# A DLRM tower on one core: products written to HBM in 136-byte pieces and read back whole, instead of written whole and read back in 136-byte pieces

## The reference, cut to what matters

```python
e = stack([tbl_f[ids[:, f]] for f in range(26)], axis=1)      # B, 26, 64
x = layer_norm(dense_t @ Wd.T, gd, bd)                        # B, 128
y = layer_norm(einsum('bnd,ed->bne', e, Ws), gs, bs)          # B, 26, 128
y = layer_norm(einsum('bne,pn->bep', y, Wsi), gsi, bsi)       # B, 128, 32
T = concatenate([x[:, None, :], swapaxes(y, 1, 2)], axis=1)   # B, 33, 128
Z = einsum('bnd,bmd->bnm', T, T)                              # B, 33, 33
z = layer_norm(Z[:, TRIL_I, TRIL_J] @ Wl.T, gl, bl) * mask    # B, 512, first 384 in use
h = maximum(concatenate([z, r_dense_t], 1) @ W_top1 + b_top1, 0)
y = maximum(h @ W_top2 + b_top2, 0) @ W_top3                  # B, 1
```

## Time and profile before

| what | us |
|---|---|
| median of 3 runs | 965.37 |
| lowest and highest run | 953.86 and 973.7 |
| span of the profiled execution, first to last instruction | 583.2 |
| PE busy in it | 520.8 |
| PE weight loads busy | 438.6 |
| DVE busy | 443.4 |
| POOL busy | 398.6 |
| ACT busy | 273.3 |

### The profile page before, as it was taken

One profiled execution on the slowest core, in us unless ns is written; L12 is line 12 of the kernel. 1 busy time (PEld: TensorE's weight loads), 2 busy tenths in 40 slices (PEclk: granted clock), 3 DMA queues, 4 the chain that ended last, 5 costly groups with the idle time before them and its releaser, 6 DMA issues.

```text
span 583.2 us, 19038 instructions
## 1 busy us (share of the span) xinstructions
PE 520.8 (89%) x7293; PEld 438.6 (75%) x7293; DVE 443.4 (76%) x862; ACT 273.3 (47%) x647; POOL 398.6 (68%) x420
## 2 busy tenths in 40 slices
PE   2469689999999999999998989999998999899786
PEld 1456568888787878887797868788787878788575
DVE  5488888888787878787787878787887888787611
ACT  1124354544545463645554464645545454646321
POOL 6777776777777777777777777777777777774000
PEclk9988989999999999999999999999999999999889
DMA  3534435454444436354543545354544444353410
GB/s 90 154 121 125 58 64 68 72 64 74 52 70 61 63 64 65 63 66 72 56 70 58 65 63 65 64 66 72 56 68 63 64 67 56 65 70 52 47 23 2
DMA packets 97305, 39.04 MB, mean 67 GB/s; under 512 B 77313, under 2 KB 89217, under 8 KB 97281
## 3 DMA queue, kind: packets, MB, share of 16 engines
q1 hardware_dynamic: 83970, 25.07, 30.7%
q0 software_dynamic: 13312, 13.66, 13.5%
HBM read 29.76 MB, written 8.92 MB: 66 GB/s over the span
## 4 chain that ended last, share of the span: by engine, by line
POOL 56%; issue 19%; DMA 10%; PE 10%; DVE 2%; ACT 1%; SPq 0%; POOLq 0%; DVEq 0%; ACTq 0%
POOL rows L452 56%; DMA rows<-in_table,index 10%; PE p_y L463 2%; PE p_u L541 1%; PE p_b L463 1%; PE p_b L480 1%; PE p_z L613 1%; PE p_b L485 1%; PE p_b L482 1%; PE p_t L516 0%; PE p_q L552 0%; PE p_y L577 0%; DVE ut_low L1000 0%; PE p_q L701 0%; PE p_y L670 0%
## 5 line engine op out<-in xcount | busy, mean ns | idle before, releaser
L452 POOL DMA_INDIRECT rows<-in_table,index x416 | 398.4, 958 | 134.0 <-issue 122.9
L541 PEld LDWEIGHTS p_u<-wsi_c,rows_n 128*128 128x128 f32 x512 | 83.3, 195 | 2.8
L1046 DVE TENSOR_TENSOR feat<-p_y,y_rs 128x1024 f32<-128x1024 f32 x64 | 78.4, 1225 | 9.1 <-DVE y_rs L1043 3.7
L1033 DVE TENSOR_REDUCE y_sum<-y_sq 128x32 f32<-128x1024 f32 x64 | 77.9, 1217 | 6.5 <-ACT y_sq L800 2.3
L541 PE MATMUL p_u<-wsi_c,rows_n 128*128 128x192 f32 (+4 forms) x512 | 82.8, 306 | 0.0
L1000 DVE TENSOR_TENSOR ut_low<-p_u,ut_high 128x512 fp32r<-128x512 f32 x64 | 44.1, 689 | 32.3 <-ACT ut_high L751 32.1
L800 ACT ACTIVATE y_sq<-p_y 128x1024 f32<-128x1024 f32 x64 | 64.8, 1012 | 3.3 <-PE p_y L581 3.3
L552 PE MATMUL p_q<-gram,et 128*128 128x128 f32 x416 | 60.4, 285 | 2.7 <-ACT et L738 2.7
L738 ACT COPY et<-p_t 128x512 f32<-128x512 f32 (+1 forms) x64 | 32.2, 504 | 63.5 <-PE p_t L516 61.4
L613 PEld LDWEIGHTS p_z<-feat 128*32 128x32 f32 x4096 | 47.6, 111 | 16.8 <-issue 12.3
L613 PE MATMUL p_z<-feat 128*32 128x34 f32 x4096 | 57.4, 201 | 0.1
(11 more groups left out here) (140 smaller groups left out, 854.2 us busy)
## 6 DMA issues: line engine op xcount, KB each, us to landing
products<-zs SPq DMA_DIRECT2D x64, 136.0 KB
zb<-products SPq DMA_DIRECT2D x256, 34.0 KB
rows<-in_table,index POOLq DMA_INDIRECT x416
dense_x<-in_dense SPq DMA_DIRECT2D x16, 128.0 KB
wl<-in_Wl_rows SPq DMA_DIRECT2D x1, 1280.0 KB, 6.5
w<-in_W SPq DMA_DIRECT2D x2, 512.0 KB
masks<-in_masks SPq DMA_DIRECT2D x1, 960.0 KB, 6.7
w1z<-in_W SPq DMA_DIRECT2D x1, 768.0 KB, 4.5
```

The costliest lines, as they stand in the source:

```text
L452: pool.indirect_dma_start(out=rows[:, j, g, :], out_offset=None, in_=a["table"], in_offset=bass.IndirectOffsetOnAxis(ap=index[:, n, t, g % ...
L541: last = nc.tensor.matmul(p_u[:, NP * (lo - UH * of):NP * (hi + 1 - UH * of)], rows_n[:, t, :, :].rearrange("r h d -> r (h d)"), wsi_c[:, ...
L1033: nc.vector.tensor_reduce(y_sum[:], y_sq[:], AX, ALU.add).then_inc(y_summed, 1)
L1046: nc.vector.tensor_tensor(feat[:, (j - 1) % UB, :, 2:SLOTS], p_y[:].rearrange("e (b p) -> e b p", p=NP), y_rs[:].unsqueeze(2).to_broadcast ...
```

## The change

The samples of a batch get another order: sample 32 u + 4 g + s of a batch is now sample (g, s) of unit u. A unit's 32 samples are then 32 neighbouring partitions of `zb`. `scratch` gets the shape (batch, unit, g, 128, 34), so that a sample's 32 rows of 34 floats lie together in HBM. The read back of a unit is one DMA of 32 pieces of 4,352 bytes in place of four DMAs of 256 pieces of 136 bytes. The store of a unit, 128 pieces of 1,088 bytes before, becomes 1,024 pieces of 136 bytes. ACT's wait on `zb_in` counts 16 a batch and quarter in place of 64, its copy of x to `feat` goes in the new order, and the host orders `ids` to match.

```diff
-    scratch = nc.dram_tensor("products", (NB, 128, GB, SLOTS), F32, kind="Internal").ap()
+    scratch = nc.dram_tensor("products", (NB, UB, GU, 128, SLOTS), F32, kind="Internal").ap()
...
             def read_quarter(of, quarter):
 
                 sp.sem_inc(read_begun, 1)
-                for s in range(SQ):
-                    at = 32 * s + GU * quarter
-                    sp.dma_start(plain[at:at + GU],
-                                 scratch[of, 32 * s:32 * s + 32, GU * quarter:GU * quarter + GU, :].rearrange("p g c -> g p c")
-                                 ).then_inc(zb_in[quarter], 16)
+                sp.dma_start(zb[SU * quarter:SU * quarter + SU, 0:ZROW],
+                             scratch[of, quarter].rearrange("g (s p) c -> (g s) (p c)", s=SQ)).then_inc(zb_in[quarter], 16)
...
-                        sp.dma_start(scratch[of, :, GU * quarter:GU * quarter + GU, :],
+                        sp.dma_start(scratch[of, quarter].rearrange("g r c -> r g c"),
                                      zs[:, j % 2]).then_inc(z_stored[j % 2], 16)
...
                         for quarter in range(UB):
-                            act.wait_ge(zb_in[quarter], 64 * i)
+                            act.wait_ge(zb_in[quarter], 16 * i)
...
-                        nc.scalar.copy(feat[:].rearrange("e u (s g) c -> e c s u g", s=SQ)[:, 0],
-                                       p_a[:, 128:256].rearrange("e (s u g) -> e s u g", s=SQ, u=UB)).then_inc(xt_ready, 1)
+                        nc.scalar.copy(feat[:].rearrange("e u (s g) c -> e c u g s", s=SQ)[:, 0],
+                                       p_a[:, 128:256].rearrange("e (u g s) -> e u g s", s=SQ, u=UB)).then_inc(xt_ready, 1)
...
-    ids = x["ids"].reshape(NB, 2, 2, UB, GU, NF).transpose(0, 1, 3, 2, 4, 5).reshape(NB, 2, NT, 128).transpose(3, 0, 2, 1)
+    ids = x["ids"].reshape(NB, UB, GU, 2, 2, NF).transpose(0, 3, 1, 4, 2, 5).reshape(NB, 2, NT, 128).transpose(3, 0, 2, 1)
```

## The result

The changed kernel takes **987.98 us** (median of 4 runs, 983.56 to 990.93), the kernel before 968.26 us (4 runs beside it, 953.86 to 973.7). The ratio is **1.028, 95% interval 1.020 to 1.035**: slower, by about 20 us. 962 was forecast and 982 was the range's upper end, so time and direction were both missed. A ratio in this document is that of each kernel's faster runs, those within 1.5% of its quickest, so it can differ from the ratio of the medians.

A forecast was written before the change was run, and what follows sets the result against it. The prediction took POOL's gather pace as the bound. From the 583.2 us span it took 2.8 us of POOL's waits and 0.3 at the end, giving 580.1, and carried 382.2 us outside: 962 us, range 948 to 982.

The forecast's parts named there:

- What bounds the kernel now: First step: POOL's gathers, at least 1.249 us apart, set 98% of the time up to 531.9 us.
- the 382 us: Time between the 583.2 us span and the timed median, taken to lie outside the span and carried unchanged.
- It can give POOL at most 4.5 us: Bound on what changed DMA queues could save POOL in late gathers in the steady part: 4.5 us.
- Reads, 0.5 us: Read back of a unit as 4,352-byte pieces: 0.5 us of transfer in place of 3.0, not on the path by itself.
- Stores, 3.0 us: Store of a unit as 1,024 pieces of 136 bytes: taken as 3.0 us, between 0.5 and 6.0.
- SP's queue, 4.4 us from store to read: SP's wait between a unit's store and read grows from 1.94 to 4.4 us, at no cost.
- The end, hidden: Last store and read land at 560.1, hidden by 3.4 us behind ACT's L718, which ends at 563.48.
- POOL's waits for landings below 5 us: Sign in the profile after: POOL's idle for DMA at its gathers, line 449, below 5 us in total.
- Rival 3: Small HBM writes are slow, hold DMA engines and make gathers late: 14 to 109 us, middle 1025 us; chance 0.10.
- Rival 2: New stores run earlier in each turn and may meet waited-for gathers: 14 us more, 979 us; chance 0.12.
- Rivals 1 and 4: POOL's waits come from elsewhere, nothing gained, 965 us, chance 0.22; or more comes back, some 10 us, 955 us, 0.08.
- Rival 5: The read's 4,352-byte pieces are cut small again, so DMA bursts double: 979 us; chance 0.03.

The follow-up runs named there:

- e3: Changed kernel with its new small-piece store but the four old small reads a unit, products permuted: 943.25 us, ratio 1.038 to the kernel before (921.12).
- e4: Changed kernel with the old store of 1,088-byte pieces and the new large read, products permuted: 998.38 us, ratio 1.103 to the kernel before.
- e5: Kernel before with one matmul a unit in place of its 64 products, transfers unchanged: 852.7 us (unedited kernel before 921.12).
- e8: Kernel before with two added waits, on POOL's gathers and PE's products, that keep gathers and products apart: 849.23 us (without them 918.55).
- e1: Kernel before, unedited, timed and profiled again: 974.82 us (934.6 to 993.73, 10 runs).
- e10: Old store with the new large read in the changed kernel, as e4, run again in another group: 990.21 us (kernel before 918.55).
- e12: Changed kernel plus the four old small reads a unit into an unused tile, with ACT waiting for them too: 951.02 us (kernel before 969.23).
- e14: Changed kernel with one added wait: POOL starts a unit's gathers only after the products two units back: 791.56 us, ratio 0.821 to the kernel before.
- e6: Changed kernel with one matmul a unit in place of its 64 products, transfers unchanged: 837.35 us (unedited kernel before 921.12).
- e7: Changed kernel with two added waits, on POOL's gathers and PE's products, that keep gathers and products apart: 827.89 us (kernel before 918.55).

## Why the prediction was wrong

**The step that failed is the first: "What bounds the kernel now".** "98% of the time up to 531.9 us is POOL's own pace" is true of the execution in the earlier trace rows and of no timed one. The sign was in the table: 583.2 us of span against a 965 us median. I wrote that "the 382.2 us between span and median hold no instruction that changes, so I carry them". Every later run shows 1.8 to 1.9 us outside the span. The prediction named both halves of this as what would prove it wrong, the 382 us and a PE that "loses time that I have not seen". In the timed executions POOL stands still for 511 us before its gathers, 385 of them for a DVE result, PE idles 253 us before the products, and what counts is how much of PE's work falls in bursts of gathers.

**"It can give POOL at most 4.5 us"** was the bound of the gain for the same wrong regime. For the loss the prediction said "What it can take is not bounded this way", and that is where the +20 us went: through the large read, to PE's crawl (e3, e4 and the sign that turns in e5 to e8), a path that no term of the sum had. How the large read does it stays open.

**Sizes of the parts**, by rows of the changed kernel. SP's queue in the steady part, then the last store and read; ACT's copy at the end; the end's windows (the last two columns are DMA share and GB/s):

```profile
447.44 0.41 SPq L387 DMA_DIRECT2D products<-zs  x1
...
451.64 0.32 SPq L371 DMA_DIRECT2D zb<-products  x1
```

```profile
958.18 0.40 SPq L387 DMA_DIRECT2D products<-zs  x1
962.11 0.31 SPq L371 DMA_DIRECT2D zb<-products  x1
```

```profile
965.29 1.14 ACT L715 ACTIVATE h<-p_y,b1z 128x128 f32<-128x128 f32 x4 [4.88 <-PE p_y L460]
966.31 1.26 ACT L754 COPY zc<-zb 128x576 f32<-128x576 f32 x1
```

```profile
959.00:959.50 0.50, 0.16 (x1) 0.16 (x2) 0.29 (x1) 0.00 (x0) 0.00 (x0) 1.00 0.68 112
959.50:960.00 0.50, 0.39 (x3) 0.15 (x2) 0.00 (x0) 0.07 (x1) 0.00 (x0) 1.00 0.92 153
960.00:960.50 0.50, 0.00 (x0) 0.00 (x0) 0.00 (x0) 0.41 (x1) 0.00 (x0) 1.00 0.10 14
960.50:962.00 1.50, 1.45 (x13) 1.48 (x14) 0.00 (x0) 0.00 (x0) 0.00 (x0) 1.00 0.07 11
...
963.00:963.50 0.50, 0.50 (x7) 0.50 (x6) 0.00 (x0) 0.00 (x0) 0.00 (x0) 1.00 0.78 183
963.50:964.00 0.50, 0.50 (x7) 0.50 (x6) 0.00 (x0) 0.00 (x0) 0.00 (x0) 1.00 0.26 96
```

- *Reads, 0.5 us*: half of what they took, and of no weight in the sum. 139 KB pass from 963.0 to 964.0, so in about 1.0 us; at engine shares of 0.78 and 0.26 that is 0.52 us of all sixteen engines.
- *Stores, 3.0 us*: three times too large. 1,024 writes of 136 bytes pass in about 1.0 us at 112 to 153 GB/s, against the old reads' 3.0 us at 46. Most of that is the number of engines at work: the store takes 0.85 us of all sixteen (shares 0.68, 0.92 and 0.10), the four small reads 1.1 (0.37 over 3.0 us). By the Trainium skill, DMA: Bandwidth & Descriptors, section Why a DMA increments its semaphore by 16 and not by 1, a copy is spread over the largest number of engines up to 16 that divides the slowest dimension on both sides. That is 16 for the store and 8 for the small reads, and the prediction's estimate from it was 1.5 us. The trace agrees: eight of sixteen engines could show no share above 0.5, and the store shows 0.92, the reads 0.37. That estimate was the nearer one.
- *SP's queue, 4.4 us from store to read*: 4.2 in the steady part and 3.9 at the end, right only in sum, since 1.0 of it is pieces moving. At the end the pieces have passed by about 960.5 and SP issues the read at 962.11, with the engines at a share of 0.07 in between: the wait goes on after the data. SP waits 115.1 us in 35 waits for the store, 3.3 each (before 1.7).
- *The end, hidden*: right. The last read's data has passed at about 964, and ACT's L754 starts at 966.31 behind L715, not behind the transfer.
- *POOL's waits for landings below 5 us*: 3.4 us in 3 waits, but no hit: the kernel before as it is timed has only 1.6 us in 5 (e1), not the 7.9 of the earlier trace rows, so there was nothing to gain.

**Rivals.** Rival 3, slow small writes, gave the right sign, but not by its mechanism: the writes pass in 1.0 us, POOL waits 3.4 us in all for landings, and the small-piece store costs nothing measurable beside the large read. Why it costs 22 us beside small reads (e3) is open. Rival 2, "bunched at the wrong moment" (979 us), is nearest in kind, but had DMAs bunching against gathers; what bunches are the gathers against PE. Rivals 1 and 4 fell with their base. Rival 5 is excluded by the read's 1.0 us; pieces cut small would have kept the old 3.0.

**Shown**: the regime (e1), that the cost lies with the read more than the store (e3, e4, e10), that added small reads with a wait for them speed up the changed kernel (e12), that POOL's gate gives 18% (e14), and that the change's sign turns where the products don't crawl (15 us faster in e5 and e6, 21 in e7 and e8). **Argued only**: that small reads help by splitting bursts. e3 and e12 have fewer long bursts, but e1 has as many as the changed kernel and still varies from 934 to 994 us, and in e5 and e6, with 13 and 16 long bursts (limit 2.5 us), the one with more is the faster. By which wait the reads act was not followed. The gains of 15 and 21 us are not taken apart either. **Open**: why PE crawls while gathers are issued, and why one execution ran 583.2 us with POOL issuing all the time and no crawl.

## What to carry to other kernels

Compare the profiled execution's span with the timed median before anything else: here a gap of 40% meant that the trace showed another regime, and no sum made on it held. Where two engines take turns, look at what sets the length of the turns; one wait that stops an engine from running ahead was worth far more here (18%) than the transfers changed, and an edit that makes transfers quicker can lose. A count that rests on a limit, as that of long bursts does, has to be made with a second limit before it is believed. A half of a change that is measured by itself (e4, 10% slower) tells more than the sum of its parts worked out on paper.

## What the runs showed of the hardware

- While POOL issued indirect DMAs every 1.25 us, PE issued its matmuls in dribbles: 64 small ones that take 0.77 us with POOL silent took 14.9 us (511.52 to 526.43), and ACT took up a result of PE's 4.5 us after its end, having idled for it 2.67 us. It isn't bound to one instruction (e6), it began at a granted clock of 1.00, and it isn't there in the 583.2 us execution, where POOL issued at the same pace.
- PE's granted clock was 1.00 (2.4 GHz) when the crawl began, 0.50 (1.2 GHz) in the 5 us of full work behind it (526 to 531), and 0.785 over the span; in e14, where PE idles less, 0.87, and 1.00 through the steady part of the 583.2 us execution. PE's busy time for the same matmuls went from 520.8 to 654.8 us, so 134 us of the 403 between the two spans is matmuls that run longer.
- 1,024 writes of 136 bytes to HBM from 128 partitions passed in about 1.0 us at shares up to 0.92, as many reads of 136 bytes in four DMAs of 8 partitions in 3.0 us at a share of 0.37.
- The kernel before had the same program run at a span of 583.2 and of 982.0 us.
